# Packing the queries through a scratch in device memory, and the row of maxima issued by ScalarE

## What is computed

```python
x = x + tanh(g_xattn[0]) * attention(_layernorm(x), ctx, mask, ...)   # 16 heads of 32, 128 keys per batch
x = x + tanh(g_ffn[0]) * ffn(_layernorm(x), ...)                      # 512 -> 2048 (silu) -> 512, dequantized weights

# inside attention:
q = (xn @ w_q).reshape(B, N1, HEADS, HEAD_DIM).transpose(0, 2, 1, 3)
attn = jnp.einsum('bhqd,bhkd->bhqk', q, k) * SCALE
attn = jnp.where(mask == 0, MASK_FILL, attn)
attn = jax.nn.softmax(attn, axis=-1)
out = jnp.einsum('bhqk,bhkd->bhqd', attn, v)
return out.transpose(0, 2, 1, 3).reshape(B, N1, C) @ w_proj + b_proj
```

## Time and profile before

| | us |
|---|---|
| median of 3 runs | 1189.59 (1185.5 to 1190.39) |
| the profiled execution, its own time | 1189.94 |
| its span in the trace | 1188.1 |
| TensorE busy | 1105.6 (93%) |
| VectorE busy | 632.5 (53%) |
| ScalarE busy | 390.4 (33%) |
| GpSimd busy | 341.4 (29%) |
| mean granted TensorE clock | 0.974 of full speed |

### The profile page before, as it was taken

How to read it: one execution, slowest core, us unless ns; L and a number is a source line. 1 busy time by engine, 2 the same in 40 slices (tenths; PEclk the granted TensorE clock), 3 DMA queues, 4 the chain that set the end, 5 groups by cost and what they waited for, 6 DMA issues and landing times.

```text
span 1188.1 us, 15790 instructions
## 1 busy us (share of the span) xinstructions
PE 1105.6 (93%) x5433; PEld 848.2 (71%) x5433; DVE 632.5 (53%) x1039; ACT 390.4 (33%) x614; POOL 341.4 (29%) x344
## 2 busy tenths in 40 slices
PE   4778998999899767999999999999999999999998
PEld 3455666666566445888888888888888888888887
DVE  5667786787887437776235235335235335334312
ACT  3467675667667522341111111111111111111110
POOL 4446565566675423112102102002012012012000
PEclk9889999999999869999999999999999999999999
DMA  7534545545544457900100100100200200200000
GB/s 252 138 88 109 142 111 150 140 119 147 152 122 108 131 158 249 289 1 36 36 1 22 50 1 6 66 1 0 71 0 0 71 0 1 71 1 1 36 1 36
DMA packets 56571, 92.45 MB, mean 78 GB/s; under 512 B 12952, under 2 KB 14144, under 8 KB 56000
## 3 DMA queue, kind: packets, MB, share of 16 engines
q1 hardware_dynamic: 54024, 87.35, 25.2%
q10 hardware_dynamic: 2488, 4.34, 1.2%
HBM read 47.34 MB, written 16.78 MB: 54 GB/s over the span
## 4 chain that ended last, share of the span: by engine, by line
PE 60%; DVE 1%; issue 0%; ACT 0%; DVEq 0%
PE ps_y L220 10%; PE ps_y L219 10%; PE ps_z L1220 10%; PE ps_z L1221 10%; PE ps_z L1222 10%; PE ps_y L218 10%; PE ps_h L1234 1%; DVE x_in L1340 0%; DVE x L1303 0%; DVE y_hi L1280 0%; DVE w_lo L176 0%; DVE w_f L170 0%; ACT w_hi L161 0%; DVE y_lo L1282 0%; DVEq L47 0%
## 5 line engine op out<-in xcount | busy, mean ns | idle before, releaser
L1280 DVE CAST y_hi<-y_f 128x512 fp32r<-128x512 f32 x128 | 63.2, 494 | 391.6 <-ACT y_f L1255 391.6
L1255 ACT ACTIVATE y_f<-ps_y,cols 128x512 f32<-128x512 f32 x128 | 87.9, 687 | 553.0 <-PE ps_y L220 553.0
L1220 PE MATMUL ps_z<-w_hi,y_hi 128*128 128x512 f32 x512 | 203.2, 397 | 3.0 <-DVE w_lo L176 3.0
L218 PE MATMUL ps_y<-xt_hi,w_hi 128*128 128x512 f32 x512 | 202.0, 395 | 3.0 <-PEq L255 3.0
L220 PE MATMUL ps_y<-xt_hi,w_lo 128*128 128x512 f32 x512 | 203.4, 397 | 0.0
L219 PE MATMUL ps_y<-xt_lo,w_hi 128*128 128x512 f32 x512 | 202.9, 396 | 0.0
L1222 PE MATMUL ps_z<-w_hi,y_lo 128*128 128x512 f32 x512 | 200.6, 392 | 0.0
L1221 PE MATMUL ps_z<-w_lo,y_hi 128*128 128x512 f32 x512 | 200.6, 392 | 0.0
L218 PEld LDWEIGHTS ps_y<-xt_hi,w_hi 128*128 128x128 f32 x512 | 96.2, 188 | 26.2 <-issue 3.4
L1220 PEld LDWEIGHTS ps_z<-w_hi,y_hi 128*128 128x128 f32 x512 | 96.6, 189 | 23.8 <-DVE w_lo L176 3.4
L219 PEld LDWEIGHTS ps_y<-xt_lo,w_hi 128*128 128x128 f32 x512 | 96.6, 189 | 22.7
(11 more groups left out here) (161 smaller groups left out, 1592.9 us busy)
## 6 DMA issues: line engine op xcount, KB each, us to landing
q_pack<-q_hi SPq DMA_DIRECT2D x256, 64.0 KB, 2.0
x_in<-in_x SPq DMA_DIRECT2D x8, 1024.0 KB, 6.3
q_pack<-q_lo SPq DMA_DIRECT2D x128, 64.0 KB, 2.0
x_res<-in_x SPq DMA_DIRECT2D x32, 256.0 KB, 3.3
x_dram<-x_out SPq DMA_DIRECT2D x32, 256.0 KB, 3.4
q_raw<-in_L_ffn_fc_q SPq DMA_DIRECT2D x6, 1024.0 KB, 18.9
s_raw<-in_L_ffn_fc_scales SPq DMA_DIRECT2D x6, 1024.0 KB, 17.3
x_in<-x_dram SPq DMA_DIRECT2D x4, 1024.0 KB, 5.4
```

What stands on the lines that cost most here:

```text
L218: nc.tensor.matmul(out, s_hi, m_hi, start=(k == 0), stop=False)
L1220: nc.tensor.matmul(ps_z[t][:, :], hi, w2_hi[:, f, :], start=(f == 0), stop=False)
L1255: nc.scalar.activation(y_f[f % 2][:, :], ps_y[f % 2][:, :], ACT.Silu, bias=b1_c[:, f:f + 1]).then_inc(y_f_ready, 1)
```

## The change

The queries no longer go from tile to tile. SP stores `q_hi` and `q_lo` of a unit whole into a scratch in device memory (two transfers of 128 x 512, as soon as each part is made), and in the following step loads them into `q_pack` with three transfers, one for each group of 32 rows with all four heads in it. A new pair of semaphores `q_stored` says that the store has landed, and it also frees `q_hi` and `q_lo` in place of `q_packed`. The four transfers of the row of maxima leave SP. ScalarE issues them, behind its copy of the maxima and after a wait for the end of that copy.

```diff
+    q_dram = [nc.dram_tensor(f"q_dram{n}", (2, P, CHUNK), F32, kind="Internal").ap() for n in range(2)]
...
             def step(i, k):
+                if real(i, k + 1, UNITS):
+                    pack_queries(i, k + 1)
                 if k == FIRST:
                     load_x(i, 0)
...
-                if real(i, k + 1, UNITS):
-                    pack_maxima(i, k + 1)
                 if real(i, k + 2, UNITS):
-                    pack_queries(i, k + 2)
+                    store_queries(i, k + 2)
+            def store_queries(i, k):
-            def pack_maxima(i, k):
                 v = PER * i + k
-                sp.lower_val(v + 1)
-                after(sp, max_row_ready, v + 1)
-                for j in range(HG):
-                    sp.dma_start(q_pack[k % 2][3 * HEAD:PACK, j, :].bitcast(F32),
-                                 max_row[k % 2][j:j + 1, :].bitcast(F32)).then_inc(max_packed[k % 2], 16)
+                after(sp, q_packed[k % 2], 16 * 3 * before_in_slot(i, k))
+                after(sp, q_hi_ready, v + 1)
+                sp.dma_start(q_dram[k % 2][0, :, :], q_hi[k % 2][:, :].bitcast(F32)).then_inc(q_stored[k % 2], 16)
+                after(sp, q_lo_ready, v + 1)
+                sp.dma_start(q_dram[k % 2][1, :, :], q_lo[k % 2][:, :].bitcast(F32)).then_inc(q_stored[k % 2], 16)
             def pack_queries(i, k):
                 v = PER * i + k
-                after(sp, q_hi_ready, v + 1)
-                after(sp, q_lo_ready, v + 1)
+                after(sp, q_stored[k % 2], 16 * 2 * (before_in_slot(i, k) + 1))
                 after(sp, s_done, HG * (v - 1))
-                for n, part in enumerate((q_hi, q_lo, q_hi)):
-                    for j in range(HG):
-                        sp.dma_start(q_pack[k % 2][head_rows(n), j, :].bitcast(F32), part[k % 2][head_rows(j), :].bitcast(F32)
-                                     ).then_inc(q_packed[k % 2], 16)
+                for n, part in enumerate((0, 1, 0)):
+                    sp.dma_start(q_pack[k % 2][head_rows(n), :, :].bitcast(F32),
+                                 q_dram[k % 2][part, :, :].rearrange("(j d) n -> d j n", j=HG)).then_inc(q_packed[k % 2], 16)
...
                 nc.scalar.copy(max_row[k % 2][:, :], ps_max[1][0:HG, :]).then_inc(max_row_ready, 1)
+                after(act, max_row_ready, v + 1)
+                for j in range(HG):
+                    act.dma_start(q_pack[k % 2][3 * HEAD:PACK, j, :].bitcast(F32),
+                                  max_row[k % 2][j:j + 1, :].bitcast(F32)).then_inc(max_packed[k % 2], 16)
```

More of the change, by code:

```diff
@@ L241, in attention @@
     B, D, KB, FB, TT, KEYS, NCHUNK, SCALE = (g(n) for n in ("B", "D", "KB", "FB", "TT", "KEYS", "NCHUNK", "SCALE"))
-    maxima = g("maxima")
+    maxima, q_dram = g("maxima"), g("q_dram")
     (x_in, x_norm, xt_f, xt_hi, xt_lo, stats, mean_var, ln_a, ln_r1, ln_b, ln_c, ln_r2, ln_s2, ln_r, u_scale, lng_c, lnb_c,
@@ L326, in attention @@
         res_loaded = [sem("res_loaded0"), sem("res_loaded1")]
-        q_packed, max_packed = ([sem(f"{name}{n}") for n in range(2)] for name in ("q_packed", "max_packed"))
+        q_stored, q_packed, max_packed = ([sem(f"{name}{n}") for n in range(2)] for name in ("q_stored", "q_packed", "max_packed"))
         (stats_some, stats_ready, ln_step, rstd_ready, norm_ready, xt_turned, xt_f_ready, xt_hi_ready, xt_lo_ready,
@@ L412, in step @@
                     sp.dma_start(target, x1_out[t % 2][:, :]).then_inc(x1_stored[t % 2], 16)
-                if real(i, k + 1, UNITS):
-                    pack_maxima(i, k + 1)
                 if real(i, k + 2, UNITS):
-                    pack_queries(i, k + 2)
-            def pack_maxima(i, k):
+                    store_queries(i, k + 2)
+            def store_queries(i, k):
                 v = PER * i + k
-                sp.lower_val(v + 1)
-                after(sp, max_row_ready, v + 1)
-                for j in range(HG):
-                    sp.dma_start(q_pack[k % 2][3 * HEAD:PACK, j, :].bitcast(F32),
-                                 max_row[k % 2][j:j + 1, :].bitcast(F32)).then_inc(max_packed[k % 2], 16)
+                after(sp, q_packed[k % 2], 16 * 3 * before_in_slot(i, k))
[3 more added lines that the diff above has]
+                sp.dma_start(q_dram[k % 2][1, :, :], q_lo[k % 2][:, :].bitcast(F32)).then_inc(q_stored[k % 2], 16)
             def pack_queries(i, k):
                 v = PER * i + k
-                sp.lower_val(v + 1)
-                sp.lower_val(HG * (v - 1))
-                after(sp, q_hi_ready, v + 1)
-                after(sp, q_lo_ready, v + 1)
+                after(sp, q_stored[k % 2], 16 * 2 * (before_in_slot(i, k) + 1))
                 after(sp, s_done, HG * (v - 1))
-                for n, part in enumerate((q_hi, q_lo, q_hi)):
-                    for j in range(HG):
-                        sp.dma_start(q_pack[k % 2][head_rows(n), j, :].bitcast(F32), part[k % 2][head_rows(j), :].bitcast(F32)
-                                     ).then_inc(q_packed[k % 2], 16)
+                for n, part in enumerate((0, 1, 0)):
+                    sp.dma_start(q_pack[k % 2][head_rows(n), :, :].bitcast(F32),
+                                 q_dram[k % 2][part, :, :].rearrange("(j d) n -> d j n", j=HG)).then_inc(q_packed[k % 2], 16)
             def pack_keys():
@@ L510, in scores @@
                 if j == 0:
-                    after(pe, q_packed[k % 2], 16 * 3 * HG * (before_in_slot(i, k) + 1))
+                    after(pe, q_packed[k % 2], 16 * 3 * (before_in_slot(i, k) + 1))
                     after(pe, max_packed[k % 2], 16 * HG * (before_in_slot(i, k) + 1))
@@ L665, in take_queries @@
                 after(act, q_done, v + 1)
-                after(act, q_packed[k % 2], 16 * 3 * HG * before_in_slot(i, k))
+                after(act, q_stored[k % 2], 16 * 2 * before_in_slot(i, k))
                 nc.scalar.activation(q_hi[k % 2][:, :], ps_qm[:, :], ACT.Identity, scale=SCALE).then_inc(q_hi_ready, 1)
@@ L793, in queries_lo @@
                 after(dve, q_hi_ready, v + 1)
-                after(dve, q_packed[k % 2], 16 * 3 * HG * before_in_slot(i, k))
+                after(dve, q_stored[k % 2], 16 * 2 * before_in_slot(i, k))
                 nc.vector.scalar_tensor_tensor(out=q_lo[k % 2][:, :], in0=ps_qm[:, :], scalar=SCALE,
```

## The result

The changed kernel takes 1274.53 us, median of 3 runs (1273.4 to 1275.43), against 1189.59. The ratio is 1.0723, with a 95% interval of 1.0683 to 1.0764: 85 us slower. The forecast was 1257 with a range of 1205 to 1285.

The account below looks back on a forecast made before the run. It took a loop of turn, copy, probabilities, head 2 and TensorE's work as the bound, with SP full. 10.35 + 2.31 delay + 1.3 clock = 13.96 us a unit: +72.5 over 30, -5.5 at the end, 1257 us, range 1205 to 1285.

Parts of the forecast that it names:

- SP's relief: SP, full before, issues 7 instead of 18 transfers a step; TensorE's waits and their clock stretches go, some 23 us.
- the faster rival: ScalarE hands the four issues to hardware and goes on at once; only SP's gain remains: 1167 us, chance 0.09.
- the loop: Turn of maxima, copy, first probabilities, head 2, TensorE's work to the next turn: 10.35 us a unit, no slack.
- The way through device memory at nothing: Query store, load issues and landing take 8.6 to 12 us, covered by a unit of over 10 us; nothing counted.
- The delay on ScalarE, 2.31 us a unit: Between copy and `p_f`: wait for the copy plus four issues (2.11 us) lengthen each unit; bounds 1.80 to 2.69.
- The clock, 1.3 us a unit, in 4 of 5: TensorE's longer idle time before head 2 brings half clock in 4 units of 5, 1.3 us a unit, 0 to 1.7.
- The sum: A unit takes 13.96 us, 30 units add 72.5, the end gives back 5.5: 1257 us, chance 0.57.
- VectorE's waits: TensorE's waits on VectorE for the maxima, at most 1.9 us each, are less than the delay, so VectorE catches up.
- Full clock (1218): Rival: the delay on ScalarE is there, but TensorE's clock holds; 12.66 us a unit, 1218 us, chance 0.23.
- The rival that ScalarE hands its issues off at once: ScalarE goes on without delay after the copy; the unit stays at 10.35 us, 1167 us in all, chance 0.09.
- The one by which the transfers are late: Queries land late through device memory, TensorE waits before head 0 as before: near 1190 to 1200 us, chance 0.04.
- the two ways below 1205: Issues on ScalarE handed off at once (1167 us, chance 0.09); query transfers late (1190 to 1200 us, 0.04).

Follow-up runs that it names:

- e1: Changed kernel with only the four transfers of the row of maxima given back to SP, behind its query stores; device memory path stays: 1168.68 us.
- e3: Changed kernel with ScalarE's wait and four issues moved behind the eight probability instructions of the step: 1171.18 us.
- e4: Changed kernel with ten extra matmuls, result never read, on TensorE in front of head 2: 1239.09 us.
- e2: Kernel before with only the row of maxima moved to ScalarE, behind its copy and a wait; queries still go tile to tile: 1282.45 us.
- e5: Changed kernel with SP issuing the row of maxima again, ScalarE keeping only the wait for its copy's end: 1172.67 us.
- e6: Changed kernel with the four transfers of the row of maxima joined to one of four rows, still on ScalarE: 1185.3 us.

## Why the prediction was right, and where its sizes were off

**What bounds the kernel before.** SP's relief was put at 23 us (the faster rival, 1167); e1, which is that rival's condition brought about in another way, gave 1168.7, 19 us below before. That the loop sets the pace and ScalarE's busy share hides it is shown by e3: same engine, same issues, another place, 103 us.

**The way through device memory at nothing.** Shown by e1, where the queries go this way and no wait of TensorE for them is left. The page of the profile after has (KB each, us to landing):

```profile
q_pack<-q_dram SPq DMA_DIRECT2D x96, 256.0 KB, 3.9
...
q_dram<-q_lo SPq DMA_DIRECT2D x32, 256.0 KB, 3.1
```

Store 3.1, three issues 1.3 and landing 3.9 are 8.3 us, a little under the 8.6 to 12 that were set against a unit. In the changed kernel too no wait of TensorE for the queries is left.

**The delay on ScalarE, 2.31 us a unit.** It was 3.14 to 3.25 less 0.48, 2.66 to 2.77 in most units: the forecast was too small by 0.4, and the delay lies at or just above its upper bound of 2.69. Two terms were mis-sized. The four issues took 2.44 and not 2.11: the price of SP's full queue, which I had only as a bound, holds here, while the two `ACTq` rows that I went by were shorter. And from the end of the last issue to `p_f` 0.20 us pass in the steps in the middle and 0.09 in the others, where 0.05 were taken. In three units the four issues took 2.9 to 3.0 us though SP issued nothing then; why is open.

**The clock, 1.3 us a unit, in 4 of 5.** The direction and the share were right: the clock fell in 24 of 30 units. That the share came out exactly is luck: it was taken from four idle times, three followed by half clock and one not. In 15 units the price was about right too: five of them took 14.66 to 14.69 us, 1.6 above the unit at full clock, and a little less was lost where half clock began while TensorE still idled (14.48 and 14.35). What was mis-sized are the 9 others, in which TensorE worked longer at half clock than the 3.2 us I priced (5.2 us in the one shown). The mean interval less a unit at full clock is 14.57 - 13.11 = 1.46 us, rather too little, as the first units have less work; the run with extra matmuls gives 1.2 back. The forecast of 1.3 was a little low.

**The sum.** Forecast 10.35 + 2.31 + 1.3 = 13.96 a unit, measured 14.57. The 0.61 are 0.45 of delay (a unit at full clock took 13.11, not 12.66) and 0.16 of clock, and 30 times that is 18 us, about the whole of the difference to 1257. The end of the stage gave back 9.0 instead of 5.5, and the start took 2.7 that I had not counted. That VectorE's waits vanish under the delay came out (13.4 to 4.0).

**The rivals.** Full clock (1218) didn't happen; e4, with ten matmuls more and the clock held in all but the first units, is at 1239, in the main since the delay is larger than forecast. The rival that ScalarE hands its issues off at once fell in this place and is half true in another, as e3 shows. The one by which the transfers are late fell with e1. The chances behind the range don't add up as written: the two ways below 1205 had 0.09 and 0.04, more than 1 in 10, and the three slower ones 0.87, not 0.86.

The Trainium skill (Perfetto Trace Analysis, DMA Optimizations) says to spread transfers over the engines that can issue them where making descriptors is the bottleneck. Here the place on such an engine decides: with the same spread the kernel takes 1274.5 us in one place and 1171.2 in another.

The Trainium skill also tells of a lock on the block that makes the descriptors (Perfetto Trace Analysis, DMA Instruction — HWDGE). In ScalarE's issues it didn't show: its four took 2.44 us with SP idle (195.96 in the changed kernel) and 2.44 beside issues of SP (195.54 in e2). SP's beside them took 0.46 to 0.83 us each, but single ones took up to 1.26 where ScalarE issued nothing (192.94 in e2), so that can't be put down to a lock either:

```profile
194.87 2.09 SPq L434 DMA_DIRECT2D q_pack<-q_hi  x3
197.01 0.61 SPq L405 DMA_DIRECT2D x_res<-in_x  x1
```

**A version that beats both.** e1, 1168.7 us, 1.5% under the kernel before and 8.3% under the changed one; e3 is 2.5 us behind it.

## What to carry to other kernels

An engine that is busy for a third of the span can still set the pace, if a loop of waits runs through it: before work is moved onto it, look at what is queued behind the new instructions and who waits for that. Issuing a DMA is such work; here each issue cost 0.6 us of the issuing sequencer, and four of them in each unit cost 106 us in one place and 3 in another. Add to a new wait of TensorE what it does to the clock: at least 35 of the 106 us here.

## What the runs showed of the hardware that was not expected

- A load of the residual took SP 0.58 us to issue when its queue was full and 0.35 in the changed kernel, a 256 KB load of queries 0.42, a store 0.32. The four of the row of maxima, 2 KB each, took 2.4 to 2.5 us in most units, on SP and on ScalarE, beside other issues or alone (e1, e2, after), and up to 3.1 in a few. Why these are not cheaper on a queue with time stays open.
- The same wait cost ScalarE 0.61 us from copy to `p_f` in the first and last steps and 0.78 in the middle ones (e5). The middle steps stand in a loop, where the counts are computed in registers; that this is the reason was not tried.
- Nearly equal idle times, 2.63 to 2.86 us in most units, were followed now by no stretch at half clock (a unit of 13.1 us), now by one that cost 1.4 to 1.6 us, and now by one that cost some 2.7 (a unit of 15.8). Idle times of 0.8 to 1.1 us (e6) brought none in any of 25 units.
